# Graph attention with a mixture of experts: target scores from windows of 32 nodes, picked by TensorE, instead of look-ups, scatters and scans

## The chip, the cores and the metric

One core of a Trainium2 chip runs the whole kernel in one launch. The metric is the device time of one execution in microseconds. DVE is VectorE, ACT is ScalarE, PE is TensorE, POOL is GpSimd, and SP is the engine that only issues DMAs. All data is float32 or int32.

## What is computed

3,125 nodes with 256 features, 50,000 edges (src, dst) sorted by dst, 8 heads of 256 channels. The part that the change touches is the first line of the attention, the score of each edge:

```python
h = (x @ W).reshape(N, H, C)                      # x: layer-normed nodes
a_src = jnp.einsum('nhc,hc->nh', h, att_src)      # 8 numbers per node
a_dst = jnp.einsum('nhc,hc->nh', h, att_dst)
e = jax.nn.leaky_relu(a_src[src] + a_dst[dst], NEG_SLOPE)
m = jax.ops.segment_max(e, dst, num_segments=N)   # softmax over the edges of a target
e = jnp.exp(e - m[dst])
denom = jax.ops.segment_sum(e, dst, num_segments=N)
alpha = e / (denom[dst] + EPS)
out = jax.ops.segment_sum(h[src] * alpha[:, :, None], dst, num_segments=N)
x = x + out.mean(axis=1) + bias
x = x + moe(layernorm(x))                         # router over 8 experts, two of them per token
```

a_dst[dst] is what the change makes in another way. `dst` is sorted, but its edges crowd on low nodes.

## The kernel before

There are NB = 392 blocks of BLK = 128 edges. Blocks are worked in nine groups (GROUP_PLAN): seven of 48 blocks, one of 32, one of 24. Four blocks are a quad. The order on each engine is written out by hand, with semaphores between engines.

**Before the groups.** SP loads the edges as 98 rows of RUN = 512 (four blocks each). PE turns them, DVE keeps `idx` (sources) and `dst_far` (mirrored targets) with an edge per partition. ACT loads W, att_src, att_dst. DVE sums W times att into `va` (`sum_va`, 8 heads times 2 halves of the features, one reduce each), takes the statistics of all 25 tiles of x (`bn_stats`), PE turns x and multiplies it with `va` (`score`), DVE scales to `score_all` (L1410). SP stores the normed x and the source scores as node_table, 264 numbers a row.

**The target scores before.** For every node, the place of its first edge is looked for: ACT counts blocks (`count_blocks`, L1218), POOL fetches for each of the 25 tiles a block of targets by an indirect DMA (L727), DVE compares it with the nodes (L1490, L1491, 3,200 columns), and POOL scatters the nodes' scores to the places of first edges in `starts_table` (L788, 25 DMAs). SP brings the table back, DVE fills each run by scans (L1602, one per head), PE turns the result (L964), ACT writes `score_d`, an edge per partition.

**The groups.** POOL's `gather` (L735) brings 128 rows of node_table for a block into the ring of 96 slots. From group 2 on it waits for `block_done`, which PE raises when a block in the slot it needs has been added. POOL's queue is: 32 gathers, 25 scatters, one look-up of start_rows (L791), 16 gathers, 48 for group 1, then for each group g `far_blocks(g - 2)` and the gathers of g. DVE's part of a group is `flags` (masks, L1619 to L1629), `scores` (L1641, waits for the gathers), a segmented softmax by scans, and `spreads` (L1758), which makes the right operand for PE's `add_block` (L973, 160 columns, two matmuls a block). ACT drains the sums (L1258).

**After the groups**: projections (L1097), router, experts (L1156, L1172), scatter-add of the results.

```python
pool.wait_ge(idx_ready, 1)
pool.wait_ge(node_scores_stored, 16)
pool.wait_ge(xn_stored, 16 * (TILES // UNROLL))
pool.wait_ge(va_summed, 2)
gather(0, 0, FIRST_GATHERS)
```

Of the kernel before, what the change touches and what calls it, by code (L numbers as in the profile page):

```python
# [41 lines left out]
TURNED_BANKS = (2, 4, 5, 6)  # L42

LOOK_UPS = ((0, 2), (2, 5), (5, 10), (10, 17), (17, 25))
FIRST_GATHERS = 32
# [19 lines left out]
def gat_moe_kernel(nc, x, src, dst, W, att_src, att_dst, gnn_bias, router_w, w1, b1, w2, b2, out):  # L65
# [29 lines left out]
    assert LOOK_UPS[-1][1] == TILES and H * CHUNKS == P and D == 2 * P and C == D and N < TILES * P  # L95
# [14 lines left out]
    score_table = nc.dram_tensor("score_table", [TILES * P, H], F32).ap()  # L110
    starts_table = nc.dram_tensor("starts_table", [EP + TILES * P, H], F32).ap()
# [19 lines left out]

    MIRROR = TILES * P - 1

    with ExitStack() as ctx:
# [11 lines left out]
        o = 0  # L146
        xn = ring[:, o:o + TILES * D].rearrange("p (t d) -> p t d", d=D)
        o += TILES * D
        W_in = ring[:, o:o + 2 * H * C].rearrange("p (k n) -> p k n", k=2)
# [5 lines left out]
        count_junk = [ring[:, o + n * NB:o + (n + 1) * NB] for n in range(2)]  # L155
        o += 2 * NB
        xT = ring[:, o:o + TILES * D].rearrange("p (t d) -> p t d", d=D)
        o += TILES * D
        reach_junk, first_home_bc, last_home_bc = (ring[:, o + n * NB:o + (n + 1) * NB] for n in range(3))
        o += 3 * NB  # L160
        assert o <= RING
# [52 lines left out]
        starts_in = arena[0:TURN_ROWS, o:o + RUN * H]  # L214
        is_before = arena[:, o:o + TILES * BLK].rearrange("p (t j) -> p t j", j=BLK)
        first_i, last_i = (arena[0:1, o + RUN * H + n * NB:o + RUN * H + (n + 1) * NB].bitcast(I32) for n in range(2))
# [3 lines left out]
        filled_in = arena[0:TURN_ROWS, o:o + RUN * H].rearrange("p (h n) -> p h n", h=H)  # L220
        node_block = arena[:, o:o + TILES * BLK].bitcast(I32).rearrange("p (t j) -> p t j", j=BLK)
        dst_keys = arena[0:TURN_ROWS, o:o + RUN].bitcast(I32)
        o += NSCAN * SCAN
# [5 lines left out]
        stage = [arena[:, o + j * STAGE:o + (j + 1) * STAGE] for j in range(ACC_RING)]  # L229
        o += ACC_RING * STAGE  # L230
        score_d = arena[0:BLK, o:o + NB * H].rearrange("p (b h) -> p b h", h=H)
        home_f, first_f, even_f, slot_f, last_home_f, extra_f, row_f = (
            arena[0:1, o + n * NB:o + (n + 1) * NB] for n in range(7))
        row_tmp = row_f.bitcast(I32)
        extra_sum = arena[0:1, o + 7 * NB:o + 8 * NB]
        o += NB * H
        assert 8 * NB <= NB * H
        assert RUN * H + 2 * NB <= SPREAD_RING * QUAD * SPREAD * H and RUN * H <= NSCAN * SCAN
        alpha = score_d

# [1901 lines left out]
```

## Time and profile before

| what | us |
|---|---|
| three timed executions, median | 1032.7 |
| lowest and highest of them | 1027.82 and 1033.31 |
| span of the profiled execution, first to last instruction | 1025.7 |
| busy in it: PE, DVE, POOL, ACT | 669.8, 680.2, 673.2, 355.3 |

For the profiled execution only the span is recorded, no time of its own. Busy time is a sum over stages with different limits. Matmuls overlap each other and their weight loads, so the time of a matmul in a row of many is the length of the row divided by their number. A float32 matmul appears as two records, a transpose as one.

### The profile page before, as it was taken

To read this page: it belongs to the slowest core of one execution; us is meant where nothing else is said; L and a number is where in the kernel's file an instruction comes from. 1 tells how busy PE (TensorE), PEld (TensorE's weight loads), DVE (VectorE), ACT (ScalarE), POOL (GpSimd) and SP (SyncE) were. 2 spreads that over 40 slices of the span, in tenths; PEclk is the share of its full clock that TensorE was granted. 3 is DMA by queue.
4 is the path that set the end of the run, shared out by engine and by line. 5 is a ranking of instruction groups with operands and counts; after the bars stand their busy time and mean duration, and the time that the engine had idled before them with its cause. 6 is when DMAs were issued, how large, how long until landed. Compare 5 with 4: busy or idle time off the path is not lost.

```text
span 1025.7 us, 15575 instructions
## 1 busy us (share of the span) xinstructions
PE 669.8 (65%) x3740; PEld 602.6 (59%) x3741; DVE 680.2 (66%) x1860; ACT 355.3 (35%) x831; POOL 673.2 (66%) x705
## 2 busy tenths in 40 slices
PE   4982012427646275471754687599999998678996
PEld 3981001327546175461654677588888887567995
DVE  6888318727757276572875778657678968775663
ACT  3720003337645364231331110023323222335664
POOL 5787777777777777777777771235073375557786
PEclk9999999978878687676876898899999999889998
DMA  9634153567867677555664456198986862366873
GB/s 347 217 80 96 24 117 103 163 223 255 260 204 241 206 249 220 168 180 156 187 182 134 142 165 254 40 337 310 346 321 225 298 230 83 80 133 99 134 130 58
DMA packets 96985, 189.62 MB, mean 185 GB/s; under 512 B 24743, under 2 KB 54802, under 8 KB 95804
## 3 DMA queue, kind: packets, MB, share of 16 engines
q0 software_dynamic: 31680, 70.52, 28.3%
q1 hardware_dynamic: 50256, 72.93, 21.0%
q10 hardware_dynamic: 14960, 45.16, 11.4%
q8 instruction: 35, 0.57, 0.2%
q14 instruction: 54, 0.44, 0.1%
HBM read 124.74 MB, written 64.74 MB: 185 GB/s over the span
## 4 chain that ended last, share of the span: by engine, by line
PE 29%; POOL 26%; DVE 19%; issue 13%; DMA 8%; ACT 1%; POOLq 1%; DVEq 1%; ACTq 0%; SPq 0%; PEldq 0%; PEld 0%
POOL ring L735 22%; PE banks L1097 12%; PE banks L973 5%; PE banks L1172 3%; PE banks L1156 3%; DMA ring<-node_table,idx 3%; POOL starts_table L788 2%; DMA out<-ring 2%; PE banks L927 2%; DVE arena L1373 2%; DMA ring<-agg_table 1%; PE banks L914 1%; DMA arena<-in_src 1%; POOL slot_table L835 1%; PE banks L1144 1%
## 5 line engine op out<-in xcount | busy, mean ns | idle before, releaser
L735 POOL DMA_INDIRECT ring<-node_table,idx x392 | 408.7, 1043 | 121.4 <-issue 115.0
L973 PE MATMUL banks<-arena,ring 128*128 128x160 f32 x1568 | 256.9, 328 | 39.3 <-ACT banks L1264 18.7
L973 PEld LDWEIGHTS banks<-arena,ring 128*128 128x128 f32 x1568 | 245.2, 212 | 51.8 <-issue 51.4
L1258 ACT COPY arena<-banks 128x400 f32<-128x400 f32 x200 | 88.4, 493 | 322.6 <-PE banks L973 204.9
L1097 PE MATMUL banks<-ring 128*128 128x256 f32 x544 | 120.5, 381 | 0.0
L849 POOL DMA_INDIRECT out<-ring x56 | 89.8, 1603 | 33.9 <-DMA out<-ring 18.0
L1097 PEld LDWEIGHTS banks<-ring 128*128 128x128 f32 x544 | 102.7, 190 | 13.2
L1758 DVE TENSOR_TENSOR arena<-hot,arena 128x640 f32<-128x640 f32 x84 | 64.6, 823 | 34.8 <-PE banks L973 34.5
L980 PE MATMUL banks<-ident,edge_e 128*128 128x128 f32 x25 | 7.2, 417 | 119.7 <-DVEq L1649 119.6
L980 PEld LDWEIGHTS banks<-ident,edge_e 128*128 128x128 f32 x25 | 3.9, 201 | 121.9 <-DVEq L1649 121.9
L1156 PEld LDWEIGHTS banks<-ring 128*128 128x128 f32 x448 | 60.6, 200 | 20.0 <-DVE ring L2022 16.8
L1156 PE MATMUL banks<-ring 128*128 128x128 f32 x448 | 63.3, 287 | 13.2 <-DVE ring L2022 13.0
L835 POOL DMA_INDIRECT slot_table<-arena,slots x50 | 57.2, 1143 | 14.5 <-issue 13.7
L1172 PE MATMUL banks<-arena,ring 128*128 x224 | 62.4, 403 | 1.5 <-issue 1.4
L1641 DVE TENSOR_TENSOR edge_z<-ring,arena 128x384 f32<-128x384 f32 (+2 forms) x9 | 4.3, 478 | 82.4 <-DMA ring<-node_table,idx 82.4
L1097 PE MATMUL banks<-ring,arena 128*128 128x256 f32 x256 | 57.0, 381 | 0.0
L830 POOL COPY arena<-tags 128x3 f32<-128x3 f32 x25 | 3.6, 194 | 80.6 <-DVEq L1910 80.6
L1262 ACT COPY banks<-zeros 128x400 f32<-128x400 f32 x100 | 50.4, 504 | 11.6 <-ACT arena L1258 10.2
L1097 PEld LDWEIGHTS banks<-ring,arena 128*128 128x128 f32 x256 | 48.4, 190 | 6.3
L2046 DVE SCALAR_TENSOR_TENSOR ring<-banks,job_w,ring 128x256 f32<-128x256 f32 x56 | 27.1, 484 | 35.8 <-PE banks L1172 29.7
L1264 ACT COPY banks<-zeros 128x400 f32<-128x400 f32 x100 | 49.7, 497 | 0.0
L1172 PEld LDWEIGHTS banks<-arena,ring 128*128 128x128 f32 x224 | 40.2, 200 | 7.1 <-issue 3.4
(411 smaller groups left out, 1183.1 us busy)
## 6 DMA issues: line engine op xcount, KB each, us to landing
agg_table<-arena ACTq DMA_DIRECT2D x100, 400.0 KB
ring<-agg_table SPq DMA_DIRECT2D x25, 1600.0 KB, 8.5
ring<-slot_table SPq DMA_DIRECT2D x56, 130.0 KB, 2.6
ring<-node_table,idx POOLq DMA_INDIRECT x392
ring<-in_x SPq DMA_DIRECT2D x8, 640.0 KB, 13.2
arena<-in_L_ffn_w SPq DMA_DIRECT2D x16, 256.0 KB, 8.7
node_table<-ring SPq DMA_DIRECT2D x5, 640.0 KB, 5.4
ring<-in_L_gnn_W ACTq DMA_DIRECT2D x1, 2048.0 KB, 9.0
```

Source lines behind the costliest of these rows:

```text
L735: pool.indirect_dma_start(rows[:, slot_of(b), :], None, node_table, bass.IndirectOffsetOnAxis(idx[:, b:b + 1], 0)).then_inc(got[got_of(g)] ...
L835: pool.indirect_dma_start(slot_table, bass.IndirectOffsetOnAxis(slots[:, k, t:t + 1], 0), tn[t % TN_RING], None).then_inc(sent[t % TN_RING ...
L849: pool.indirect_dma_start(out, bass.IndirectOffsetOnAxis(xs[j % XS_RING][:, D:D + 1].bitcast(I32), 0), ybuf[j % Y_RING], None, bounds_chec ...
L973: m = pe.matmul(columns[:, k, bass.ds(at * (UNIT * H), SPREAD * H)], lhs[:, k * P:(k + 1) * P], weights, start=False, stop=True, skip_grou ...
L1097: m = pe.matmul(bank[proj_bank(t)][:, 0:D], aggt[t % AGG_RING][:, k * H + h, :], W_sb[:, k, h * C:(h + 1) * C], start=(k == 0 and h == 0), ...
L1156: m = pe.matmul(h_bank[j % 2][:, f * P:(f + 1) * P], w1_now[j % 2][:, k, f * P:(f + 1) * P], xsT[j % 2][:, k, :], start=(k == 0), stop=(k ...
L1172: m = pe.matmul(y_bank[j % 2][:, 0:D], h_sb[j % 2][:, f, :], w2_sb[:, bass.ds(e, 1), f, :].rearrange("p e n -> p (e n)"), start=(f == 0), ...
L1258: act.copy(stage[j][:, k * SLOTS * H:(k + 1) * SLOTS * H], views[k]).then_inc(drained, 1)
L1262: act.copy(views[0], zeros[:, 0:1].to_broadcast([P, SLOTS * H]))
L1264: act.copy(views[1], zeros[:, 0:1].to_broadcast([P, SLOTS * H])).then_inc(acc_free, 1)
L1758: dve.tensor_tensor(spread[:, s:s + QUAD, :].rearrange("p s (d h) -> p s d h", h=H), hot[:, q * QUAD:(q + 1) * QUAD, :].unsqueeze(3).to_br ...
L2046: dve.scalar_tensor_tensor(ybuf[j % Y_RING], y_bank[j % 2][:, 0:D], job_w[j % 3][:, 1:2], b2_now[j % 3], ALU.mult, ALU.add).then_inc(y_rea ...
```

## The change

Nodes get windows of WIN = 32 consecutive targets, starting at every 8th node, in a table `windows` of 32 x 8 numbers per row. The blocks' first targets give for each of the 392 blocks a window that holds its near targets. Four indirect DMAs bring these 392 windows (128 blocks each, SETS = 4 rows of edges at a time), DVE transposes them within 32 partitions (`near`), and for each of 25 lots of 16 blocks PE shows on every partition the place of each of 512 edges within its window, DVE makes a one-hot from it, and PE multiplies the one-hot with `near`. Blocks that reach beyond a window go through a slow path that this data does not take. The counting on ACT, the look-ups, compares, scatters, and scans go. Both halves of `va` are summed first and the nodes are scored once with 16 columns. Node tiles hold consecutive rows per partition. ACT normalises 10 of the 25 tiles. The far check is asked once for all groups.

```diff
-FIRST_GATHERS = 32
+FIRST_GATHERS = 12
+STEP = 8
+WIN = 32
+SETS = 4
@@ sync
+            sp.wait_ge(rows_made, 1)
+            sp.dma_start(window_rows, row_of_window[:, 2, :]).then_inc(first_stores, 16)
             sp.wait_ge(score_ready, 1)
-            sp.dma_start(node_table[:, D:].rearrange("(t p) h -> p t h", p=P), score_all[:, :, 0:H])\
-                .then_inc(node_scores_stored, 16)
+            sp.dma_start(node_major(node_table[:, D:]), score_all[:, 0, 0:FULL, :]).then_inc(node_scores_stored, 16)
...
+            for c in range(SHIFTS + 1):
+                nodes = target_scores
...
+                sp.dma_start(node_major(nodes), score_all[:, 1, 0:FULL, :]).then_inc(target_scores_stored, 16)
@@ gpsimd
-            for t0, t1 in LOOK_UPS:
...
-                    pool.indirect_dma_start(node_block[:, t, :], None, block_rows,
-                                            bass.IndirectOffsetOnAxis(block_of_i[:, t:t + 1], 0)).then_inc(node_block_in, 16)
...
             gather(0, 0, FIRST_GATHERS)
-            for t in range(TILES):
-                pool.indirect_dma_start(starts_table, bass.IndirectOffsetOnAxis(starts_at[:, t:t + 1], 0),
-                                        score_all[:, t, H:2 * H], None).then_inc(starts_sent, 16)
...
+            pool.wait_ge(target_scores_stored, 16 * 2 * (SHIFTS + 1))
+            pool.wait_ge(window_at_in, 16 * WINDOW_LOADS)
+            pool.wait_ge(rel_turned, 2)
+            for s in range(WINDOW_TURNS):
+                pool.indirect_dma_start(window[:, s, :, :].rearrange("p w h -> p (w h)"), None, windows,
+                                        bass.IndirectOffsetOnAxis(window_at[:, s:s + 1], 0)).then_inc(windows_in, 16)
             gather(0, FIRST_GATHERS, GB)
-            pool.wait_ge(steps_ready, 1)
-            gather(1, 0, GB)
-            for g in range(2, GROUPS - 1):
-                far_blocks(g - 2)
-                gather(g, 0, blocks_of(g))
+            pool.wait_ge(far_known, 2)
+            is_far = pool.value_load(far[0:1, 0:1], min_val=0, max_val=2 * NS)
+            with pool.If(is_far < 1):
+                pool.sem_inc(beyond_ready, 1)
+                gather(1, 0, GB)
+                for g in range(2, GROUPS - 1):
+                    gather(g, 0, blocks_of(g))
+                gather(GROUPS - 1, 0, blocks_of(GROUPS - 1))
@@ tensor
-            for h in range(H):
-                pe.wait_ge(filled_ready, h + 1)
...
+            def show_lot(n):
+                if n >= 2:
+                    pe.wait_ge(hot_window_ready, n - 1)
+                part = slice(n * SETS // WIN * WIN, min(TURN_ROWS, n * SETS // WIN * WIN + WIN))
+                pe.matmul(bank[LOT_BANKS[n % 2]][:, 0:RUN], lot_sel[part, n % STEP * P:(n % STEP + 1) * P],
+                          in_window[part, :], start=True, stop=True).then_inc(lot_shown, 1)
+
+            def score_lot(n):
+                pe.wait_ge(hot_window_ready, n + 1)
...
+                for j in range(TURN_BLOCKS):
+                    m = pe.matmul(to[:, :, j, :], hot_window[n % 2][:, j * BLK:(j + 1) * BLK],
+                                  near[:, n * TURN_BLOCKS + j, :, :], start=True, stop=True)
+                m.then_inc(lot_scored, 1)
+
+            pe.wait_ge(rel_read, 3)
+            show_lot(0)
+            pe.wait_ge(near_ready, SETS)
+            for n in range(LOTS):
+                if n + 1 < LOTS:
+                    show_lot(n + 1)
+                score_lot(n)
@@ vector
+            center_va()
...
+            dve.wait_ge(score_done, 1)
+            scale_scores(0)
+            scale_scores(1)
...
-            for n, op in enumerate((ALU.is_lt, ALU.is_le)):
-                link(dve.tensor_tensor(is_before, node_block, node_bc, op))
-                link(dve.tensor_reduce(inside[:, n, :], is_before, AX_X, ALU.add))
...
-            for h in range(H):
-                dve.tensor_tensor_scan(filled_in[:, h, :], same_node, values[:, h, :], 0.0, ALU.mult, ALU.add)\
-                    .then_inc(filled_ready, 1)
...
+            for q in range(SETS):
+                here = slice(q * WIN, (q + 1) * WIN)
+                dve.transpose(near[here, :, q, :].rearrange("p (s x) h -> p h s x", s=WINDOW_TURNS),
+                              window[here, :, :, :].rearrange("p s w h -> p h s w")).then_inc(near_ready, 1)
+
+            for n in range(LOTS):
+                dve.wait_ge(lot_shown, n + 1)
+                if n >= 2:
+                    dve.wait_ge(lot_scored, n - 1)
+                dve.tensor_scalar(hot_window[n % 2], bank[LOT_BANKS[n % 2]][:, 0:RUN], in_lot[:, 0:1], None, ALU.is_equal)\
+                    .then_inc(hot_window_ready, 1)
```

On POOL, where group 0's gathers stand, the queue before reads as follows (`arena` and `ring` are the two large rooms in SBUF that all tiles share; a number behind x counts equal instructions):

```order
L735 DMA ring<-node_table,idx 128x264 x32
L788 DMA starts_table<-score_all,starts_at 53376x8 x25
L791 DMA start_rows<-score_table,start_idx 98x8
L735 DMA ring<-node_table,idx 128x264 x64
L740 TENSOR_LOAD far
```

And of the change, at the same place (L829 brings the windows, L777 is `gather`):

```order
L777 DMA ring<-node_table,idx 128x264 [waits pool_chain,va_summed,xn_stored,first_stores,node_scores_stored,idx_ready]
L777 DMA ring<-node_table,idx 128x264 x11
L829 DMA arena<-windows,window_at 128x256 [waits rel_turned,window_at_in,target_scores_stored]
L829 DMA arena<-windows,window_at 128x256 x3
L777 DMA ring<-node_table,idx 128x264 x36
L835 TENSOR_LOAD far [waits far_known]
```

26 DMAs between the gathers of group 0 have become four.

On PE, behind the two small transposes L1010, which end the preparation, the order now is (L1017 is `show_lot`, its output 512 columns; L1027 is `score_lot`, 32 columns as 4x8 apart):

```order
L1010 MATMUL banks<-ident,step_cols 1x128
L1017 MATMUL banks<-arena 128x512 [waits rel_read]
L1017 MATMUL banks<-arena 128x512 [waits near_ready]
L1027 MATMUL banks<-arena 128x4x8 [waits hot_window_ready]
L1027 MATMUL banks<-arena 128x4x8 x3
L1017 MATMUL banks<-arena 128x512 [waits hot_window_ready]
L1027 MATMUL banks<-arena 128x4x8 [waits hot_window_ready]
L1027 MATMUL banks<-arena 128x4x8 x3
```

Where 32 transposes (L964) stood behind the scans, 25 shows and 100 picks stand, one show ahead of the lot that is picked.

On DVE, ahead of the flags of group 0 (L1619 before, L1699 now), before:

```order
L1594 MEMSET piece_all 8x34
L1599 COPY arena<-start_rows 98x8
L1602 SCALAR_TENSOR_TENSOR arena<-hot,arena 98x512 x8
L1619 TENSOR_TENSOR arena<-dst_scan 128x385
```

and of the change:

```order
L1669 MEMSET piece_all 8x34
L1676 STREAM_TRANSPOSE arena<-arena 32x8x128 x4
L1683 TENSOR_SCALAR arena<-banks,in_lot 128x512 x25
L1699 TENSOR_TENSOR arena<-dst_scan 128x385
```

A copy and eight scans have become four transposes and 25 compares, and group 0's flags stand behind the last compare.

## Rows read from the trace of the kernel before

**Rows 1.** The page, chain that ended last: share by engine, then by line.
```profile
PE 29%; POOL 26%; DVE 19%; issue 13%; DMA 8%; ACT 1%; POOLq 1%; DVEq 1%; ACTq 0%; SPq 0%; PEldq 0%; PEld 0%
POOL ring L735 22%; PE banks L1097 12%; PE banks L973 5%; PE banks L1172 3%; PE banks L1156 3%; DMA ring<-node_table,idx 3%; POOL starts_table L788 2%; DMA out<-ring 2%; PE banks L927 2%; DVE arena L1373 2%; DMA ring<-agg_table 1%; PE banks L914 1%; DMA arena<-in_src 1%; POOL slot_table L835 1%; PE banks L1144 1%
```

**Rows 2.** Groups by line, POOL, 160 to 620 us (busy us, mean ns | idle before).
```profile
L735 POOL DMA_INDIRECT ring<-node_table,idx x347 | 353.8, 1020 | 107.7 <-issue 101.3 <-PE banks L973 6.4
```

**Rows 3.** Timeline of POOL (start us, duration us, instruction, idle before).
```profile
57.74 1.08 POOL L735 DMA_INDIRECT ring<-node_table,idx  x1 [0.30 <-issue]
...
106.38 1.02 POOL L788 DMA_INDIRECT starts_table<-score_all,starts_at  x1 [0.30 <-issue]
...
139.56 1.00 POOL L735 DMA_INDIRECT ring<-node_table,idx  x1 [0.31 <-issue]
...
227.83 0.95 POOL L735 DMA_INDIRECT ring<-node_table,idx  x1 [0.30 <-issue]
...
619.28 1.48 POOL L735 DMA_INDIRECT ring<-node_table,idx  x1 [0.30 <-issue]
```

**Rows 4.** Scores of a group on DVE: the page's group, then the timeline.
```profile
L1641 DVE TENSOR_TENSOR edge_z<-ring,arena 128x384 f32<-128x384 f32 (+2 forms) x9 | 4.3, 478 | 82.4 <-DMA ring<-node_table,idx 82.4
...
165.26 0.56 DVE L1641 TENSOR_TENSOR edge_z<-ring,arena 128x384 f32<-128x384 f32 x1 [1.32 <-DMA ring<-node_table,idx]
...
229.47 0.43 DVE L1641 TENSOR_TENSOR edge_z<-ring,arena 128x256 f32<-128x256 f32 x1 [14.00 <-DMA ring<-node_table,idx]
```

**Rows 5.** Timeline of DVE before the groups.
```profile
14.99 0.41 DVE L1395 CUSTOM_DVE_ANT_0 ring<-ring 128x256 f32<-128x256 f32 x1
...
22.35 0.08 DVE L1395 DVE_READ_ACCUMULATOR2_ANT va<- 128x1 f32 x1
...
24.80 8.26 DVE L1431 BATCH_NORM_STATS2 stats<-ring 128x6 f32<-128x256 f32 x25
33.09 0.20 DVE L1434 TENSOR_TENSOR mean<-stats 128x25 f32<-128x25 f32 x1
...
57.11 0.51 DVE L1457 TENSOR_SCALAR home<-arena 1x392 int32<-1x392 int32 x1
...
69.15 3.49 DVE L1490 TENSOR_TENSOR arena<-arena,node_keys 128x3200 f32<-128x3200 int32 x1 [0.24 <-DVE arena L1481]
...
86.28 0.34 DVE L1510 CAST extras<-arena 1x392 int32<-1x392 f32 x1
...
104.04 0.57 DVE L1569 COPY ring<-banks 128x392 f32<-128x392 f32 x1
...
149.10 0.21 DVE L1599 COPY arena<-start_rows 98x8 f32<-98x8 f32 x1 [37.23 <-DMA arena<-starts_table]
...
159.39 0.56 DVE L1619 TENSOR_TENSOR arena<-dst_scan 128x385 f32<-128x385 int32 x1 [1.01 <-PE banks L964]
...
162.79 1.16 DVE L1629 TENSOR_TENSOR hot<-ids,dst_rel 128x960 f32<-128x960 f32 x1
```

**Rows 6.** Timeline of PE; the second 195.09 row is cut at 200 us.
```profile
57.25 21.50 PE L927 MATMUL banks<-va,ring 128*128 128x8 f32 x100 [0.27 <-DVE va L1405]
78.68 4.29 PE L954 MATMUL banks<-arena,ones_row 1*128 1x392 f32 x6
...
195.09 7.13 PE L973 MATMUL banks<-arena,ring 128*128 128x160 f32 x32 [2.63 <-DVE arena L1758]
...
195.09 5.13 PE L973 MATMUL banks<-arena,ring 128*128 128x160 f32 x19 [2.63 <-DVE arena L1758]
...
727.86 13.91 PE banks L1097 x64
...
893.46 1.16 PE L1156 MATMUL banks<-ring 128*128 128x128 f32 x8 [2.35 <-DVE ring L2022]
```

**Rows 7.** The chain in order of time: start us, us, what.
```profile
52.27 3.94 DMA node_table<-score_all
```

**Rows 8.** A stretch of 4 us: PE busy (records), PEclk, DMA share, GB/s.
```profile
892.00:896.00 4.00, 2.40 (x14) 1.00 0.62 132
```

More of the change, by code:

```diff
@@ L154, in gat_moe_kernel @@
         o += C
[L155 to L161, printed above, removed]
+        zero_part = ring[:, o:o + SHIFTS * TABLE_ROWS * WIN * H // P]
+        o += SHIFTS * TABLE_ROWS * WIN * H // P
+        assert o <= (SLOT0 + GB) * ROW
         AGG = 2 * H * P
@@ new lines, in _ @@
+            is_far = pool.value_load(far[0:1, 0:1], min_val=0, max_val=2 * NS)
[5 more added lines that the diff above has]
+                gather(GROUPS - 1, 0, blocks_of(GROUPS - 1))
+            with pool.Else():
+                pool.wait_ge(near_ready, SETS)
+                for b in range(NB):
+                    pool.indirect_dma_start(beyond_scores[:, b, :], None, target_scores,
+                                            bass.IndirectOffsetOnAxis(beyond_row[:, b:b + 1], 0)).then_inc(windows_in, 16)
+                pool.wait_ge(windows_in, 16 * (WINDOW_TURNS + NB))
+                pool.wait_ge(round_read, ROUNDS)
+                pool.tensor_tensor(score_d, score_d, beyond_scores, ALU.add).then_inc(beyond_ready, 1)
+                pool.wait_ge(beyond_ready, 1)
+                gather(1, 0, GB)
+                for g in range(2, GROUPS - 1):
+                    far_blocks(g - 2)
+                    gather(g, 0, blocks_of(g))
+                gather(GROUPS - 1, 0, now)
+                far_blocks(GROUPS - 3)
+                gather(GROUPS - 1, now, blocks_of(GROUPS - 1))
+                far_blocks(GROUPS - 2)
+                far_blocks(GROUPS - 1)
@@ L1424, in _ @@
             dve.wait_ge(last_row_done, 1)
-            link(dve.tensor_copy(last_i[:, :], bank[3][0:1, 0:NB]))
+            link(dve.tensor_copy(last_i[:, :], bank[0][0:1, 0:NB]))
+            for a in range(2):
+                dve.wait_ge(in_att[a], 16)
+                if a == 0:
+                    dve.wait_ge(in_W, 16)
+                for k in range(2):
+                    sum_va(a, k)
             for t in range(TILES):
@@ L1510, in _ @@
+            link(dve.tensor_copy(lot_sel.rearrange("p (x w) -> p x w", w=WIN), lot_rows[:, :].unsqueeze(2).to_broadcast([TURN_ROWS, WIN, WIN])))
+            dve.sem_inc(rel_read, 1)
+            link(dve.tensor_scalar(beyond_row, beyond_key, -1.0, float(MIRROR), ALU.mult, ALU.add))
+            dve.sem_inc(far_known, 1)
             link(dve.tensor_copy(extras[:, :], extra_f[:, :]))
```

465 lines of the change are left out of this document (248 added, 217 removed).

## The prediction

> **What bounds the kernel now.** I read the chain that ended last first. Nearly a quarter of the span on it is one line of POOL, L735, the gathers that bring 128 rows of node_table for a block of 128 edges [rows 1]. The view by lines for 160 to 620 us shows why: 347 gathers, 353.8 us busy, mean 1,020 ns, and the idle time before them is "issue" for 101.3 us and PE for 6.4 us. So a gather costs 1.02 + 0.30 = 1.32 us and almost none waits for anything [rows 2]. POOL's timeline gives its shape: first gather at 57.74 us, 32 of them; from 106.38 us the 25 scatters of starts and the one look-up of start_rows; at 139.56 us the 16 gathers that end group 0; group 2's first gather, which is the first that must wait for a freed slot, at 227.83 us; the last one at 619.28 us [rows 3]. VectorE (DVE) at the start of each group's scores (L1641) sits idle until a gather lands, 82.4 us over nine groups, 14.0 us at group 1 [rows 4]. A group takes DVE 50.2 us (165.26 to 229.47, less the 14.0 idle) and POOL 48 x 1.32 = 63.4 us. So whatever moves POOL's row of gathers moves the end, and DVE and PE can be late only until POOL starts to wait for slots. That is the quantity to follow: **when group 2's first gather can issue**, 227.83 us now.
>
> **When POOL can start.** The gathers need the nodes' scores in HBM. Before, the sums for att_src alone (16 pairs of reduce and read, 14.99 to 22.43 us) come first. Now both halves come first: DVE waits for last_row, one 392-column matmul behind idx at 15.2 us (1.43 as each of L954's [rows 6], to 16.7; the copy of it to 17.4), then 2 x 7.44 = 14.9 us, to 32.3. The 25 bn_stats (8.3) end at 40.6; the small operations on 25 columns (33.09 to 37.78, 4.7) at 45.3; centring at 45.6 [rows 5]. Only then can TensorE score. It makes 50 matmuls with 16 columns, 100 records; the 100 records with 8 columns took 21.50 us, 0.215 each, and the 128x128 weight of each is the same [rows 6]. I take 21.5, not half: to 67.2. Bound below, if the clock were at its upper level, 100 x 0.145 = 14.5. Scaling both halves 0.6 and eight operations on 98x4 at 0.2 give 69.5 us; SP sends window_rows ahead of the scores (0.4 to 0.5), and the scores need 3.94 us to land [rows 7]. First gather at about 74.3, **16.5 us later** than 57.74. DVE's 25 normalisations, 10 of them now ACT's, lie under the scoring and cost nothing; they would only if they took over 21 us.
>
> **What POOL no longer does.** The 25 dst look-ups lay ahead of 57.7 us and cost nothing once the start is set by the scores. The 26 DMAs from 106.38 to 139.56 us, 33.2 us, go; four window gathers come, 5.3 us. Their inputs are 14 tiny loads and 10 stores on SP, some 24 x 0.4 us from 72 us, landed near 87; POOL comes there at 74.3 + 12 x 1.32 = 90. Group 2's first gather has 52 + 48 = 100 DMAs ahead: 74.3 + 132 = **206.5 us**, 21.3 earlier than 227.83, if its slot is free.
>
> **When DVE reaches the picking.** From 69.5: two 98x512 operations and two small ones 1.7; the home chain (57.11 to 69.0) 11.8; two copies of relative rows out of PSUM 1.8; lot_sel (98x1024, priced by L1629's 960 columns in 1.16) and lot_rows 1.5; beyond_row 0.4: 86.7. The block from 86.28 to 102.00 us 15.7 plus two tiny ones 0.4; then 102.60 to 111.9 less one PSUM copy, 8.7: 111.5 [rows 5]. What is gone is the compare and reduce over 3,200 columns (four at 3.49 us) with the small operations behind them, and the wait of 37.2 us for starts. New are four transposes, which no row shows, of 1,024 columns: between 1.16 and twice that each. I take 1.16, since the work is a copy's: the picking starts at **116.2 us**; with the upper price at 120.8. By the Trainium skill's page Vector Engine (DVE) Microarchitecture Reference, section 3.8, a transpose sustains one element per cycle and lane; its estimate by that page would be 1.07 us each.
>
> **The picking loop, new and serial.** For each of 25 lots TensorE shows 512 columns from 32 partitions (L1017), DVE compares 128x512 out of PSUM into a one-hot, and TensorE multiplies it four times with 32 columns each (L1027). DVE's part is 0.57 x 512/392 = 0.75 us [rows 5] and lies under TensorE's, which never waits in the order shown. TensorE's part depends on its clock:
> - lower level (1.2 GHz): the three matmuls L954, with one partition and 392 columns, took 4.29 us, 3.65 ns a column; 512 columns give 1.87. Taken from the 19 records of 160 columns in 5.13 us (0.27 each, 3.4 ns a column) they give 1.73. The four picks are 8 records at 0.215, 1.72, since the weight load sets them. A lot: 3.45 to 3.59, I take 3.52 less the one show that comes early: 86.2 us in all.
> - upper level (2.4 GHz): 64 records of 256 columns in 13.91 us, 1.7 ns a column, give 0.87; eight records at 0.145 give 1.16. A lot 2.03, the loop 50 us [rows 6].
>
> Which? The PEclk column prints 1.00 for all the early part, but the durations do not: the 19 records from 195.09 us took 0.27 each and the 13 behind them 0.15 (7.13 - 5.13 = 2.00 us) [rows 6]. So the clock was at the lower level until about 200 us, through 21.5 us in which TensorE was never idle but streamed 8 columns per weight, and through the 4.3 us of 392-column matmuls on one partition. What raised it were dense 160-column matmuls on all partitions. In the loop half of the time is a stream from 32 partitions and half is weight load with 32 columns behind it. This is nearer to the first two, so I take the **lower level**. The loop ends at 202.4 us. The last one-hot is out 3.4 us before that plus 0.8; then flags of group 0, 4.6 us (159.39 to 163.95) [rows 5]; scores(0) at **204.4 us**, where it was 165.26. Group 0's gathers have landed at 146 us and wait.
>
> The Trainium skill, TensorE: Matmul & The Clock Gate, Part 1, says that the throttled state is the default and sustained activity releases it. Read plainly, a loop in which TensorE never idles would run at the upper level, and by that the sum would be the first rival's; the trace disagrees for the kinds of work in its first 200 us.
>
> **The sum.** Before, TensorE began group 0 at 195.09, 29.8 us after scores(0), and four blocks are 16 records of 0.27, 4.3 us: the first quad frees its slots 34.1 us after scores(0) [rows 4, 6]. Now 204.4 + 34.1 = 238.5 us. POOL is there at 206.5 and waits 32 us. Group 2's first gather issues at 238.5 instead of 227.83: **+10.7 us**. Does anything recover it? Group 1's DVE work starts at about 255, group 2's at 308, group 2's gathers have landed at 238.5 + 63.4 + 3 = 305, so DVE hides the rest and from group 3 on POOL sets the pace as before, 10.7 us later. The removed far_blocks checks between gathers cost nothing today (idle of POOL there is "issue"). Behind the last gather nothing changes. The profiled execution has no time recorded but its span, 1025.7; the median of the runs is 1032.7, 7.0 more, and I add the difference to it: **1043.4 us**, say 1043. Its own range: later by 2.3 for 3.59 us lots, 4.6 for the transposes and 3 for the start, less 3 to 5 the other way: 1038 to 1053.
>
> **Rivals.**
> - *The clock rises in the loop* (faster). With lots of 2.03 us and some 3 us until it has risen, scores(0) is at 171 to 173 us, its first quad frees at 206, just when POOL comes at 206.5. POOL's whole gain stays: -21, 1011.7 us. For it: TensorE is never idle in the loop, and tail rows at 60% busy keep 1.00 [rows 8]. Against it: what did not raise the clock up to 200 us. Lots of 2.03 to 2.9 us end in between. Chance 0.27. The skill's rule above is this rival.
> - *Both nearly cancel.* A lot of 3.0 us instead of 3.52 (less by 0.43 over 25, 10.7 us) puts the slot at 227.8: no change, 1033. This needs weight loads partly hidden behind the shows, or the transposes and small operations cheaper. Chance 0.15, within 0.5%.
> - *The windows come late.* SP's 24 DMAs land 15 us later than I put them. In my forecast POOL has 32 us to spare, and DVE reaches the transposes only at 111.5: no cost up to about 100 us of landing. It would cost only in the first rival, one for one. It shares the chance of the others.
> - *Slower, as forecast*, 0.58.
>
> 0.5% is 5 us, about what a measurement here can tell from no change. The range takes in the first rival's 1011.7 and the upper bounds: 1010 to 1053.
>
> **What would show it.** First gather at 72 to 77 us. 50 scoring matmuls in some 21 us. The record groups L1017 at 1.7 to 1.9 us a matmul and L1027 at 0.215 a record; 0.87 and 0.14 mean the first rival. The loop from about 116 to 202. scores(0) near 204, and a gap of some 30 us before POOL's 101st DMA, ended by PE; no such gap if I am wrong. DVE idle before the second group's scores should be near 0 instead of 14.0. The last gather at about 630 instead of 619.28. The forecast fails first if the lots cost under 3.0 us, or if the scores land far from 74 us in a kernel in which POOL doesn't wait.

## The result: 2.6% slower, and the profile after

The changed kernel takes 1057.41 us (median of four executions, 1057.21 to 1058.53), the kernel before 1031.16 in the same comparison (1027.82 to 1033.31): ratio 1.0262, interval 1.0238 to 1.0287. Forecast were 1043 and a range of 1010 to 1053. Slower came true, by 26.2 us where the forecast had 10.7, and the time lies 4.4 us above the range. The profiled execution has a span of 1056.3 us and took 1058.53.

The page's chain that ended last, by engine and by line (line numbers of the changed kernel: L777 is the gathers, L1044 the accumulation of groups, L1017 the shows, L1027 the picks):

```profile
PE 41%; DVE 30%; issue 8%; POOL 8%; DMA 6%; ACT 2%; DVEq 1%; ACTq 1%; POOLq 1%; SPq 0%; PEldq 0%; PEld 0%
PE banks L1168 12%; PE banks L1044 9%; POOL ring L777 7%; PE banks L1017 5%; PE banks L1027 4%; PE banks L1243 3%; PE banks L1227 3%; DMA out<-ring 2%; DMA ring<-node_table,idx 2%; PE banks L973 2%; DVE arena L1443 2%; DVE ring L1464 1%; DVE arena L1758 1%; DMA ring<-agg_table 1%; DVE arena L1676 1%
```

POOL's gathers had 22% of the chain [rows 1] and now have 7%. Shows and picks, which did not exist, have 9%. POOL's timeline, with the same points as [rows 3]: first gather, first gather of windows, group 2's first gather, the last gather.

```profile
74.80 1.24 POOL L777 DMA_INDIRECT ring<-node_table,idx  x1 [58.33 <-DMA node_table<-score_all]
...
90.95 0.96 POOL L829 DMA_INDIRECT arena<-windows,window_at  x1 [0.30 <-issue]
...
249.88 1.67 POOL L777 DMA_INDIRECT ring<-node_table,idx  x1 [48.11 <-PE banks L1044]
...
647.33 1.44 POOL L777 DMA_INDIRECT ring<-node_table,idx  x1 [0.30 <-issue]
```

Of POOL's gathers the view by lines has this for 160 to 650 us, the answer to [rows 2]:

```profile
L777 POOL DMA_INDIRECT ring<-node_table,idx x330 | 341.5, 1035 | 148.4 <-issue 94.2 <-PE banks L1044 54.2
```

The idle time put down to PE has grown from 6.4 to 54.2 us, nearly all of it in one place: POOL arrived at group 2's first gather at 249.88 - 48.11 = 201.8 us, 26 us earlier than it issued that gather before, and then waited 48.11 us for PE to free the slot. PE's timeline shows what PE was doing (start, duration, number of records):

```profile
45.64 20.66 PE L973 MATMUL banks<-va,ring 128*128 128x16 f32 x96 [9.75 <-DVE va L1473]
...
120.46 2.07 PE L1017 MATMUL banks<-arena 32*128 32x512 f32 x2 [9.13 <-DVE arena L1676]
122.46 1.92 PE L1027 MATMUL banks<-arena 128*128 128x32 f32 x8
124.31 2.07 PE L1017 MATMUL banks<-arena 32*128 32x512 f32 x2
...
210.93 3.62 PE L1027 MATMUL banks<-arena 128*128 128x32 f32 x16
...
245.31 5.38 PE L1044 MATMUL banks<-arena,ring 128*128 128x160 f32 x24 [2.33 <-DVE arena L1838]
```

From one show to the next 124.31 - 120.46 = 3.85 us pass, 2.00 for the show and 1.85 for the picks. The loop lasts from 120.46 to 214.55, 94.1 us, without a gap. DVE's timeline has the four transposes ahead of it and the scores of groups 0 and 1 behind it:

```profile
111.93 8.48 DVE L1676 STREAM_TRANSPOSE arena<-arena 32x1024 f32<-32x1024 f32 x4
...
216.28 0.56 DVE L1721 TENSOR_TENSOR edge_z<-ring,arena 128x384 f32<-128x384 f32 x1
...
265.34 0.43 DVE L1721 TENSOR_TENSOR edge_z<-ring,arena 128x256 f32<-128x256 f32 x1
```

Group 0's scores start at 216.28 us instead of 165.26 [rows 4], group 1's no longer wait for their gathers (14.0 us before). The view by stretches, for the loop, gives the clock (PE busy, PEld, DVE, ACT, POOL with their counts, PEclk, DMA share, GB/s):

```profile
120.00:214.00 94.00, 93.54 (x247) 55.97 (x247) 21.18 (x31) 3.61 (x6) 62.12 (x65) 0.50 0.36 96
```

PEclk is 0.50 throughout, 1.2 GHz, though PE was busy for 93.54 of 94.00 us.

### The profile page after: what moved, and what is told of

The parts are those of the page before. It is cut to its first block, busy times and chain, and to the rows that moved or that the text cites. A ratio compares the mean times of both kernels' runs of the same rounds, so it can differ in the third digit from the quotient of the medians.

```text
span 1056.3 us, 15692 instructions
## 1 busy us (share of the span) xinstructions
PE 734.8 (70%) x3858; PEld 632.4 (60%) x3859; DVE 677.4 (64%) x1866; ACT 328.9 (31%) x740; POOL 615.8 (58%) x642
## 4 chain that ended last, share of the span: by engine, by line
PE 41%; DVE 30%; issue 8%; POOL 8%; DMA 6%; ACT 2%; DVEq 1%; ACTq 1%; POOLq 1%; SPq 0%; PEldq 0%; PEld 0%
PE banks L1168 12%; PE banks L1044 9%; POOL ring L777 7%; PE banks L1017 5%; PE banks L1027 4%; PE banks L1243 3%; PE banks L1227 3%; DMA out<-ring 2%; DMA ring<-node_table,idx 2%; PE banks L973 2%; DVE arena L1443 2%; DVE ring L1464 1%; DVE arena L1758 1%; DMA ring<-agg_table 1%; DVE arena L1676 1%
## 5 line engine op out<-in xcount | busy, mean ns | idle before, releaser
L777 POOL DMA_INDIRECT ring<-node_table,idx x392 | 402.0, 1025 | 225.3 <-issue 112.4
L1044 PE MATMUL banks<-arena,ring 128*128 128x160 f32 x1568 | 258.9, 329 | 39.5 <-ACT banks L1334 20.1
L1044 PEld LDWEIGHTS banks<-arena,ring 128*128 128x128 f32 x1568 | 246.9, 213 | 52.2 <-issue 51.7
L1027 PEld LDWEIGHTS banks<-arena 128*128 128x128 f32 x200 | 44.5, 328 | 36.1 <-issue 36.1
L1683 DVE TENSOR_SCALAR arena<-banks,in_lot 128x512 f32<-128x512 f32 x25 | 18.8, 751 | 72.6 <-PE banks L1017 72.6
L1017 PE MATMUL banks<-arena 32*128 32x512 f32 (+1 forms) x50 | 51.8, 1137 | 9.1 <-DVE arena L1676 9.1
L1332 ACT COPY banks<-zeros 128x400 f32<-128x400 f32 x100 | 50.4, 504 | 12.4 <-ACT arena L1328 11.2
L1303 ACT COPY arena<-banks 128x512 f32<-128x512 f32 (+1 forms) x7 | 3.8, 546 | 160.2 <-PE banks L1027 160.2
```

The lines of the kernel that those rows point to most:

```text
L777: pool.indirect_dma_start(rows[:, slot_of(b), :], None, node_table, bass.IndirectOffsetOnAxis(idx[:, b:b + 1], 0)).then_inc(got[got_of(g)] ...
L1017: pe.matmul(bank[LOT_BANKS[n % 2]][:, 0:RUN], lot_sel[part, n % STEP * P:(n % STEP + 1) * P], in_window[part, :], start=True, stop=True).t ...
L1027: m = pe.matmul(to[:, :, j, :], hot_window[n % 2][:, j * BLK:(j + 1) * BLK], near[:, n * TURN_BLOCKS + j, :, :], start=True, stop=True)
L1044: m = pe.matmul(columns[:, k, bass.ds(at * (UNIT * H), SPREAD * H)], lhs[:, k * P:(k + 1) * P], weights, start=False, stop=True, skip_grou ...
L1332: act.copy(views[0], zeros[:, 0:1].to_broadcast([P, SLOTS * H]))
```

## The experiments

All profiled executions can be put on one line each. "Issue" is the start of group 2's first gather, "wait" POOL's idle time just ahead of it, "rest" the span less issue. The kernel before was executed again beside each set of variants (medians 1031.01 to 1032.88 us), and each ratio is to those executions.

| kernel | issue | wait | last gather | span | rest | median us | ratio |
|---|---|---|---|---|---|---|---|
| before | 227.83 | 0.30 | 619.28 | 1025.7 | 797.9 | 1031.16 | 1 |
| before_again | 226.50 | 0.30 | 620.76 | 1030.1 | 803.6 | 1031.77 (one) | |
| changed | 249.88 | 48.11 | 647.33 | 1056.3 | 806.4 | 1057.41 | 1.0262 |
| bf16_shows | 215.99 | 12.34 | 613.17 | 1022.7 | 806.7 | 1023.95 | 0.9919 |
| four_lots | 205.64 | 0.30 | 600.05 | 1009.5 | 803.9 | 1011.19 | 0.9793 |
| dense_before | 247.35 | 45.70 | 644.37 | 1051.8 | 804.5 | 1054.03 | 1.0207 |
| show_98 | 240.36 | 38.76 | 635.44 | 1047.6 | 807.2 | 1048.23 | 1.0155 |
| moved | 235.24 | 35.84 | 630.85 | 1039.8 | 804.6 | 1042.29 | 1.0112 |
| bf16_98 | 206.31 | 1.88 | 602.24 | 1014.0 | 807.7 | 1012.91 | 0.9822 |
| bf16_98_moved | 203.09 | 0.30 | 598.05 | 1006.8 | 803.7 | 1009.82 | 0.9801 |
| source_first | 202.22 | 7.62 | 597.06 | 1009.6 | 807.4 | 1011.02 | 0.9807 |
| source_first_fp32 | 245.54 | 53.02 | 641.46 | 1052.1 | 806.6 | 1053.89 | 1.0215 |
| dense_in_loop | 228.45 | 25.53 | 624.25 | 1033.3 | 804.9 | 1039.95 (of three) | 1.0076 |
| source_first_19 | 198.40 | 0.30 | 594.54 | 1005.7 | 807.3 | 1005.82 | 0.9753 |

**bf16_shows.** The type of the shows' two operands is changed; VectorE has one more operation, which writes the rows a second time as bf16.

```diff
-        lot_sel = arena[0:TURN_ROWS, o:o + WIN * WIN]
+        lot_sel = arena[0:TURN_ROWS, o:o + WIN * WIN // 2].bitcast(BF16)
+        in_window_b = sb("in_window_b", [TURN_ROWS, RUN], BF16)
...
-                          in_window[part, :], start=True, stop=True).then_inc(lot_shown, 1)
+                          in_window_b[part, :], start=True, stop=True).then_inc(lot_shown, 1)
```

> The picking is the same, but lot_sel and the rows that it shows are bf16 (0 and 1; positions in a window up to 31 and everything outside it stay apart in bf16). Theory A (the loop's length passes one to one to the slot of group 2's first gather, until POOL's own arrival at 201.8 us binds): a show, 2.00 us now in two records, becomes one record of 0.45 to 1.0 us, a lot 2.3 to 2.85 instead of 3.85; the loop shortens by 25 to 38 us, the slot comes free at 211 to 225 us, and the run takes 1019 to 1032 us. Theory B (what is lost is not the loop but the later and slower row of gathers behind it): under 8 us gained, over 1049. Theory C (hand-overs between TensorE and VectorE set a lot, not the streams): a lot stays over 3.3 us, over 1043.

Measured 1023.95 us, ratio 0.9919 (0.9899 to 0.9939): 33.5 us off the changed kernel, and 0.8% faster than the kernel before. Two rows of PE's timeline:

```profile
123.44 0.60 PE L1019 MATMUL banks<-in_window_b,arena 32*128 32x512 bf16 x1
123.98 1.92 PE L1029 MATMUL banks<-arena 128*128 128x32 f32 x8
125.83 0.60 PE L1019 MATMUL banks<-in_window_b,arena 32*128 32x512 bf16 x1
```

A show costs 0.54 us instead of 2.00, a lot 2.39. Over 25 lots that is 36.5; the issue moved by 33.9 and the span by 33.6. The issue passes to the end one to one: theory A. By the Trainium skill, FP8 and Floating Point Precision, TensorE Precision Notes, true FP32 takes four passes through the array; 2.00 to 0.54 is a factor of 3.7 here, and between show_98 and bf16_98 below it is 4.6 (1.85 to 0.40): four lies between the two.

**four_lots.** 4 of the 25 lots are picked, and every block gets scores of those four.

```diff
+    FEW = 4
...
-            for n in range(LOTS):
+            for n in range(FEW):
```

> Only 4 of the 25 lots are picked, and all blocks get those scores (the rest of the picking is left out). Theory A: the loop takes 15 us, scores(0) is at about 138, the first quad frees before POOL comes, POOL's gap goes, group 2's first gather issues at about 202, 48 us earlier than now and 26 earlier than in the kernel before. The end moves by the same 48: about 1010 us (1005 to 1014). Theory B (the gathers' row behind it is slower in this kernel, whatever the loop does): the row still takes 397 us instead of 391, which is in that number; if it falls back to 391, about 1003. Rival: VectorE's group 1 or the later groups bind once POOL is early, and less than 30 of the 48 us arrive: over 1027.

1011.19 us, ratio 0.9793 (0.9770 to 0.9815). The wait is gone, POOL issues at 205.64 as soon as it arrives, and 44.2 us of issue became 46.8 of span. Nothing else became the bound on the way down to 1011 us. The row of gathers from issue to the last one took 394.4 us, between the two figures of theory B.

**dense_before.** Useless matmuls in PE's idle time: 12 ahead of the transposes of step_cols, 5 behind the first show.

```diff
+            def fill(count):
+                pe.wait_ge(rel_read, 2)
+                for _ in range(count):
+                    pe.matmul(bank[7][:, 0:RUN], ident[:, :], ident[:, :].unsqueeze(1).to_broadcast([P, 4, P]), start=True, stop=True)
...
+            fill(12)
...
             show_lot(0)
+            fill(5)
```

> 12 extra matmuls of 512 columns on 128 partitions stand in TensorE's queue before its transposes of step_cols, and 5 behind the first show, in stretches in which TensorE is idle; their results are overwritten. Theory A (dense work on all partitions raises TensorE's clock, the loop's own work is what can't): the granted clock rises to the upper level during the 12, and the first lots take about 2 us; then it either stays (loop 50 us, slot free at 205, run 1013 to 1018 us) or falls back within some lots (loop 85 to 94, run 1048 to 1057). Rival (nothing before 200 us raises the clock, whatever the work): a lot stays at 3.85, 1057 us, and the extra matmuls take 1.9 to 2.0 us each; should they run over the 120.5 at which the loop can start, it is slower by that.

1054.03 us, ratio 1.0207 (1.0178 to 1.0237): the second case of theory A, in which the clock falls back. PE alone by stretches (busy, PEclk, DMA share, GB/s):

```profile
84.00:88.00 4.00, 4.00 (x7) 0.50 0.77 188
90.00:99.00 9.00, 7.82 (x19) 1.00 0.62 120
...
120.70:122.70 2.00, 2.00 (x10) 1.00 0.34 99
126.00:212.00 86.00, 86.00 (x229) 0.50 0.36 98
```

and its timeline at the start of the loop:

```profile
120.67 1.12 PE L1023 MATMUL banks<-arena 32*128 32x512 f32 x2 [2.13 <-DVE arena L1683]
121.72 1.08 PE L1033 MATMUL banks<-arena 128*128 128x32 f32 x8
122.73 1.43 PE L1023 MATMUL banks<-arena 32*128 32x512 f32 x2
124.10 1.92 PE L1033 MATMUL banks<-arena 128*128 128x32 f32 x8
```

Under the useless matmuls the clock rose to the upper level (2.4 GHz) between 88 and 90 us, and under the second set again before the loop. The first lot took 122.73 - 120.67 = 2.06 us, close to the 2.03 that the prediction worked out for the upper level. In the second lot the clock fell, and it did not rise again in 86 us in which PE had no idle time at all. So in this execution the loop's own work neither raised the clock nor kept it. The Trainium skill, TensorE: Matmul & The Clock Gate, Part 1, says that sustained activity releases the throttle; this stretch disagrees, for this kind of activity.

**dense_in_loop.** More work instead of less: 5 of these useless matmuls ahead of the loop, and one in every lot (`fill` now takes the bank as its second argument).

```diff
+            fill(5, 6)
             pe.wait_ge(near_ready, SETS)
...
                     show_lot(n + 1)
+                fill(1, 6)
                 score_lot(n)
```

> The changed kernel with more work, not less: 5 useless matmuls of 512 columns on 128 partitions ahead of the loop, and one in every lot between the show and the picks. At the lower clock such a matmul takes 2 us, a lot 5.5, the loop 138 and the run about 1100. If dense work in each lot is enough to hold the upper level that the 5 reach, a show takes 1.0, the useless one 1.0, the picks 1.0: a lot of 3.0 us, shorter than the 3.85 without it, the slot free at 228 to 232 us and the run at 1035 to 1040, although TensorE computes more. In between if the clock comes and goes.

1035.15 us in the profiled execution, 1039.95 and 1041.56 in two more, and 1093.92 in a fourth; the table has the median of the first three. The rows of one lot and the next show:

```profile
123.69 1.12 PE L1021 MATMUL banks<-arena 32*128 32x512 f32 x2
124.75 1.12 PE L1006 MATMUL banks<-ident 128*128 128x512 f32 x2
125.71 0.97 PE L1031 MATMUL banks<-arena 128*128 128x32 f32 x8
126.61 1.12 PE L1021 MATMUL banks<-arena 32*128 32x512 f32 x2
```

and the stretch of the loop, PE alone:

```profile
121.00:194.00 73.00, 71.62 (x298) 1.00 0.40 110
```

With a third kind of matmul in it a lot takes 2.92 us instead of 3.85, the clock stays at 1.00 to the end of the loop, and the issue moves from 249.88 to 228.45. Computing more made the changed kernel 1.6% faster (1057.41 to 1039.95). It is nothing to build on: the execution of 1093.92 us lies near the 1100 that was expected if the clock stays down. It has no profile but its mean granted clock is recorded, 0.787 over 1092.1 us, against 0.841 over the 1033.3 us of the profiled one. An estimate: taking the loop's 73 us at 1.00 out of the latter and putting in 132 us at 0.50 gives 0.789. That fits a loop at the lower clock, but does not show in which stretch the clock was down.

**show_98.** Each show streams from 98 rows; other lots' rows are summed into it.

```diff
-                part = slice(n * SETS // WIN * WIN, min(TURN_ROWS, n * SETS // WIN * WIN + WIN))
+                part = slice(0, TURN_ROWS)
```

> Each show streams its 512 columns from 98 partitions instead of 32 (this sums rows of other lots into it, so the picking is not the reference's). If the number of partitions decides the clock: lots of 2.0 to 2.5 us, the run 1013 to 1024 us. If it does not: a show stays at 2.00 us, a lot at 3.85, the run at 1057 within 3.

Neither. The clock stayed at 0.50, and yet the run took 1048.23 us, ratio 1.0155 (1.0128 to 1.0182), 9.2 less than the changed kernel. A lot took 3.41 us instead of 3.85: its show 1.85 instead of 2.00, its picks 1.56 instead of 1.85. The weight loads (PEld) show why. The changed kernel:

```profile
128.15 0.50 PEld L1017 LDWEIGHTS banks<-arena 32*128 32x128 f32 x2
130.15 1.78 PEld L1027 LDWEIGHTS banks<-arena 128*128 128x128 f32 x8 [1.50 <-issue]
```

and this one:

```profile
130.80 0.55 PEld L1017 LDWEIGHTS banks<-arena 98*128 98x128 f32 x2
131.86 0.34 PEld L1027 LDWEIGHTS banks<-arena 128*128 128x128 f32 x1 [0.52 <-issue]
132.72 1.62 PEld L1027 LDWEIGHTS banks<-arena 128*128 128x128 f32 x7 [0.52 <-issue]
```

Behind a show from 98 rows the first weights of the picks are loaded at 131.86, while the show still streams (to 132.72). Behind a show from 32 rows they are loaded only when it is over. The changed kernel also tells that neither the strip of 32 rows nor their number below 32 matters: its shows go through rows 0 to 95 in three strips, the last one has 2 rows, and from one show to the next it is 3.84 or 3.85 us throughout (the last, 205.09 to 208.93; the show of 2 rows takes 2.00). Where between 32 and 98 rows the overlap begins was not tried. The Trainium skill, TensorE: Matmul & The Clock Gate, Part 3, says in one place that weight loads overlap running matmuls only where their row groups differ, and in another that loads into the background weight buffer are pulled ahead too. Here the 98 rows share rows with the pick's 128 as the 32 do, and one overlaps and the other does not, so the first of the two does not hold for this loop, and the measurement decides.

**bf16_98.** The same values as in bf16_shows, from all 98 rows: a selection for each lot, with zeros in the rows of the others. VectorE makes the selections earlier, ahead of its wait for the scores; its transposes start at 111.12 us instead of 111.93.

```diff
-                pe.matmul(bank[LOT_BANKS[n % 2]][:, 0:RUN], lot_sel[part, n % STEP * P:(n % STEP + 1) * P],
-                          in_window_b[part, :], start=True, stop=True).then_inc(lot_shown, 1)
+                pe.matmul(bank[LOT_BANKS[n % 2]][:, 0:RUN], sel_of(n), in_window_b[:, :], start=True, stop=True).then_inc(lot_shown, 1)
```

> The bf16 shows of the run before, now from all 98 rows (a selection for each lot, with zeros elsewhere; the same values come out). If what fp32 shows lost between 32 rows and 98 (0.43 us a lot) is the change of row shape between a show and the picks, which keeps the weights of the next pick from being loaded during the show, it is gained here too: a lot 1.95 to 2.05 instead of 2.38, the loop 8 to 11 us shorter, slot free at 205 to 208 us, and the run 1013 to 1017 us. If it was the fp32 stream itself, a lot stays at 2.3 to 2.4 and the run at 1024.

1012.91 us, ratio 0.9822 (0.9789 to 0.9855). What bf16 saves and what 98 rows save add up:

```profile
122.17 0.61 PE L1025 MATMUL banks<-arena,extra 98*128 98x512 bf16 x1
122.57 1.75 PE L1034 MATMUL banks<-arena 128*128 128x32 f32 x8
124.14 0.61 PE L1025 MATMUL banks<-arena,extra 98*128 98x512 bf16 x1
124.14 2.02 PEld L1034 LDWEIGHTS banks<-arena 128*128 128x128 f32 x8
```

A show takes 0.40 and its picks 1.57 us, a lot 1.97, 0.42 less than with 32 rows. The picks' weights begin to load at 124.14, together with the show; in bf16_shows, whose show starts at 123.44, they begin at 123.98, when it is over. So it was not the float32 stream.

**moved.** VectorE's block from even_rows to home_row_ready stands ahead of `dve.wait_ge(score_done, 1)`; no instruction is added or taken away.

> The changed kernel with VectorE's block from even_rows to home_row_ready (14.3 us, of which the home chain is 11) ahead of its wait for the scoring, where it is idle for 16.7 us. Theory A (picking starts when VectorE reaches it, and the slot follows one to one): the loop starts 12 to 14 us earlier, at 106.5 to 108.5, group 2's first gather issues at 236 to 238, the run takes 1043 to 1046 us. Rival: the windows' gathers or the scaling, now behind the block, come later and set the start: under 5 us gained.

1042.29 us, ratio 1.0112 (1.0077 to 1.0147). The transposes start at 96.98 us instead of 111.93, the issue came 14.6 earlier, and the span is 16.5 shorter. The time is 0.7 below theory A's range.

**bf16_98_moved** has both.

> Both edits together. The slot would be free at 192 to 196 us, ahead of POOL's own arrival at 202 to 206, so theory A forecasts that only what remains to POOL's arrival is gained: POOL's gap before its 101st DMA is gone, the run takes 1010 to 1013 us, as with four lots, and not the 1002 that the sum of the two gains would give. Rival: the first gather also moves, or VectorE's early start of the groups helps: under 1008.

1009.82 us, ratio 0.9801 (0.9774 to 0.9829), at the lower edge of theory A's 1010 to 1013. PE starts the loop at 104.43 and group 0's accumulation at 186.21, so the first quad is free well ahead, and POOL's row has no gap at 203.09. After bf16_98 only 1.88 us of wait was left to win, and the issue moved by 3.2, not by the 14.6 of the same edit in moved.

**before_again** is the kernel before, profiled a second time.

> The kernel before, profiled a second time. Its row from group 2's first gather to the last took 391.5 us, that of the changed kernel 397.5, of its variants 394.4 to 397.2. If that difference is scatter between executions, this one's row lies anywhere from 391 to 397; if it belongs to the program, it is 391 to 392 again, and half of a gather's 10 ns are in every group. The execution's own time is 2 to 3 us over its span; if it is 7, the bridge of 7 us that the prediction put between span and median was right.

Its row from the issue to the last gather took 394.3 us, between the 391.5 of the first profile and 394.4 to 397.5 of the others; its rest is 803.6 us against 797.9. So 5.7 us of rest are scatter between two executions of one program. It also shows a PEclk that the first profile lacks. The first printed 1.00 for all of 0 to 200 us; this one prints 1.00 up to 23 us, 0.50 for the whole of 24 to 196 us, and rises behind that, which agrees with the durations that the prediction went by. And its own time is 1.7 us over its span.

**source_first** builds on bf16_98_moved: the sources' half of `va` is scored first, so that gathers can start, the targets' half in a second pass of 50 matmuls behind it.

```diff
-FIRST_GATHERS = 12
+FIRST_GATHERS = 26
...
+            pe.wait_ge(va_ready, 3)
+            for t in range(TILES):
+                m = score(t, 1)
+            m.then_inc(score_done, 1)
...
-            for a in range(2):
-                dve.wait_ge(in_att[a], 16)
...
```

> The last run (bf16 shows from 98 rows) with the scoring in two passes: the sources' half of va is summed, centred and scored first, stored, and the gathers start; the targets' half is scored behind it into another bank, and VectorE does the window rows and the home chain in its waits for the two. Theory A (the end follows the later of two times: POOL's arrival at its 101st DMA, and the slot): the first gather issues at 57 to 60 us instead of 75, POOL arrives at 187 to 192, the loop starts near 108 and the slot is free at 193 to 197; group 2's first gather issues there, 6 to 10 us earlier than the 203 of both edits together, and the run takes 1000 to 1004 us. Rival: the longer first part of VectorE and TensorE makes the picking start later by as much (loop start at 116 or more): 1008 or over.

1011.02 us, ratio 0.9807 (0.9779 to 0.9835), no better: the expectation failed. The time is the rival's, but not its cause. The first gather came at 66.07 us, not 57 to 60, and the windows' gathers, now behind 26 others, only at 99.71. VectorE was done with its own work at 98.2, 2.6 later than in bf16_98_moved, and then waited 8.83 us for them, so the transposes started at 107.04 instead of 95.89.

**source_first_fp32** has the same two passes on the changed kernel.

> The same two passes on the changed kernel, whose shows stay fp32 from 32 rows. Theory A: the slot binds (a lot of 3.85 us, 25 times), POOL's early start is worth nothing and only becomes a longer wait (near 60 us instead of 36); since VectorE's idle time is filled as in the run that moved its block, the run takes what that one took, 1040 to 1045. Rival, the prediction's second step (a gather that starts 17 us earlier is worth up to 17 us): 1025 to 1030.

1053.89 us, ratio 1.0215 (1.0180 to 1.0251). Over the expected time, for the same cause as above (transposes at 107.24 us, where moved has 96.98). But the question is answered: POOL starts 9 us earlier than in the changed kernel, and all it gets is a longer wait, 53.02 us. Against moved the transposes start 10.3 us later and so does the issue (245.54 for 235.24), though POOL starts earlier. While the slot binds, POOL's start is worth nothing.

**source_first_19** only puts 19 of the gathers ahead of the windows' instead of 26.

> The two passes again, with 19 instead of 26 of group 0's gathers ahead of the windows' four. In the run with 26 the windows' gathers were issued at 99.7 to 103.5 us, though the targets' scores had landed near 91, and VectorE waited 8.8 us for them before its transposes. Theory A: they are issued from about 91.5 on, the transposes start at 98 to 100 instead of 107, the slot is free at 193 to 195 us, POOL arrives at 194 to 195 as before (the order of its DMAs changes, not their number), group 2's first gather issues at about 195 and the run takes 1002 to 1006 us. Rival: VectorE or the landing of the windows still holds the transposes to 104 or later: 1008 to 1011.

1005.82 us, ratio 0.9753 (0.9726 to 0.9781), the shortest time of the study. POOL's timeline:

```profile
92.81 0.95 POOL L838 DMA_INDIRECT arena<-windows,window_at  x1 [2.95 <-DMA target_scores<-score_all]
...
198.40 1.35 POOL L786 DMA_INDIRECT ring<-node_table,idx  x1 [0.30 <-PE banks L1061]
```

The transposes start at 100.25, the issue comes at 198.40 without a wait. That is 3 us later than expected, and POOL waited 2.95 us for the targets' scores.

## Why the prediction was wrong in size and right in kind

**Right.** The mechanism: the slot of group 2's first gather, held up by the loop, sets the end. The quantity to follow (the table's "rest" is 803.6 to 807.7 in all profiles but the first, for issues from 198 to 250 us). The first gather, 74.8 for 74.3. Scoring, 100 records from 45.64 to 67.15 us, 21.5 for 21.5. DVE's arrival at the transposes, 111.9 for 111.5. From scores(0) to the free slot 249.88 - 216.28 = 33.6 us for 34.1. The lower clock in the loop. That it had been the lower one until about 200 us is true of the trace it was read from; the second profile of the same kernel and that of the changed kernel show a short rise under the first transposes of x, in the changed kernel from about 20 to 27 us. VectorE's compare, 0.75 us and hidden. The windows did not come late. POOL was free earlier than put, 201.8 for 206.5 (the sum in the prediction gives 206.3), and waited 48 us, not 32.

**Wrong, term by term, in issue.**

- *The transposes.* I took 1.16 us each, "since the work is a copy's", and they took 8.48 / 4 = 2.12: 3.8 us of the sum. The upper of my two bounds, 2.32, held. The estimate of 1.07 us that the prediction took from the Trainium skill, Vector Engine (DVE) Microarchitecture Reference, section 3.8, is half of what this trace shows.
- *The lot.* "3.45 to 3.59, I take 3.52": it is 3.85, outside both bounds, 7.9 us over the loop. This is the step that failed: a show was put at 1.73 to 1.87 us and takes 2.00, four picks at 1.72 and take 1.85. I priced shows from matmuls that stand among their own kind ([rows 6], the L954 and the 160-column L973) and picks from the scoring, which never changes its shape either. A loop that alternates 32 rows with 128 pays at the change: show_98, in which the overlap is there, has 3.41 us, just under my lower bound, and bf16_98 gains nearly as much, 0.42, a second time.
- With -0.3 between the loop's end and scores(0) and -0.5 behind them, DVE's 0.4 late arrival and these two make 11.3 of the 249.88 - 238.5 = 11.4 us.

**Wrong, behind issue.** I added nothing behind it (last gather at about 630, measured 647.33), and measured are 806.4 - 797.9 = 8.5 us. The profile that I worked from had a short rest; the same program's second profile has 803.6, so 5.7 of the 8.5 are scatter, and 2.8 are within the 803.7 to 807.7 that the variants show. Whether the changed program is a little slower there stays open.

**The bridge.** To the span I added 7.0 us, the median less the span. An execution's own time is 1.7 to 2.5 us over its span, so the first profile was of an execution faster than the median. For the changed kernel the median is 1.1 over the profiled span, 5.9 less: 1043.4 + 11.4 + 8.5 - 5.9 = 1057.4. The short rest and the long bridge come from the same fast execution and nearly cancel, which was luck; of the 14.0 us that the sum was short, 11.4 lie ahead of issue. The range had a slip too: lots of 3.59 us instead of 3.52 are worth 1.7 us by the prediction's own numbers, not 2.3.

**The rivals.** The risen clock (0.27) did not come, and dense_before shows more: even when handed the upper level, the loop lost it in its second lot. Its price was right: lots of 2.06, and bf16_98_moved, in which the slot is free when POOL comes, takes 1009.8 for the 1011.7 of that rival. The cancelling (0.15) needed a lot of 3.0 us. My range took its width from bounds of prices that had one thing in common, no change of shape, and so they could not bound one that has it.

**Where the expected gain went.** POOL did become free 26 us earlier. It bought a wait, because the scores of group 0 moved from 165 to 216 us behind a loop of 94 us in float32. The idea of the change pays once the loop costs 50: 1.8% in bf16_98, and 2.5% in source_first_19, which also has VectorE's moved block and the scoring in two passes.

## What to carry to other kernels

When an engine is freed, find the next thing that it will wait for and price that before anything else; here 48 us of POOL's time turned into a wait.
## What the runs showed of the hardware that I had not expected

- A matmul that streams from 32 rows (or 2) was not overlapped by the load of the next 128-row weights, one from 98 rows was. The change costs 0.42 to 0.44 us per pair of changes, at 1.2 GHz, in float32 and in bf16.
- TensorE without any idle time can stay at 1.2 GHz for 86 us (dense_before) and fall to it from 2.4 GHz within its second lot; the same loop with one matmul of 512 columns on 128 partitions more in every lot stayed at 2.4 GHz for 73 us, in the one execution of it that was profiled.
- A VectorE transpose of 32 x 1024 float32 takes 2.12 us, where a copy that writes 98 x 1024 took 0.69 (L1579 in the same trace). Its input and output are strided; whether that is the cost was not tried.
- In the changed kernel TensorE's clock rose within 40 transposes of 128 columns (6.38 us): the first 15 records took 3.46 us, the last 20 took 2.35. The 21.5 us of scoring with 16 columns behind them stayed at a PEclk of 0.50.
